# Graph layer kernel: keys, queries and prefix ahead of the compaction, sooner normalising, Z stores in quarters, dense comparisons

## The reference

```python
h = maximum(layernorm(x), 0)
semb, oemb = h[src] @ tokeys.T, h[src] @ toqueries.T
dots = sum(semb * relations[rel] * oemb, axis=1) / 128
values = exp(dots)
fr = src + n * rel
values = values / segment_sum(values, fr)[fr]
output = segment_sum(values[:, None] * h[dst], fr).reshape(16, n, 128)
weights = einsum('rb,bij->rij', comps, bases_w)
out = x + relu(einsum('rij,rnj->ni', weights, output))
```

## Time and profile before

| what | value |
|---|---|
| median of 3 runs | 2487.49 us (2487.05 to 2491.51) |
| profiled execution, its time | 2487.54 us |
| its span in the trace | 2485.8 us |
| PE busy over the span | 1327.6 us (53%) |
| DVE busy | 1336.7 us (54%) |
| ACT busy | 454.1 us (18%) |
| POOL busy | 1613.0 us (65%) |

### The profile page before, as it was taken

The page is one execution under the profiler, slowest core; times in us unless marked ns, Lnnn a source line. Parts: engine busy times, 40 slices in busy tenths (PEclk is TensorE's granted clock), DMA queues, the critical chain, the costliest instruction groups (busy, mean ns, idle before and its releaser), DMA issues.

```text
span 2485.8 us, 30053 instructions
## 1 busy us (share of the span) xinstructions
PE 1327.6 (53%) x9063; PEld 1000.5 (40%) x9113; DVE 1336.7 (54%) x2311; ACT 454.1 (18%) x868; POOL 1613.0 (65%) x1828
## 2 busy tenths in 40 slices
PE   2888988345453535454454545463545454454443
PEld 2665666234242424334342434342434344343433
DVE  7888888474545454454545454545454444545450
ACT  3555555210101011111101010101011111111010
POOL 3122222377777777777777777777777777777775
PEclk8999999666666767676666666666767676666666
DMA  4333333122222222222222222222222222222222
GB/s 124 139 139 127 134 139 137 53 54 56 54 56 54 55 54 56 54 55 54 56 55 54 56 54 56 54 56 54 56 54 56 54 56 54 55 54 56 55 54 41
DMA packets 77959, 170.30 MB, mean 69 GB/s; under 512 B 29796, under 2 KB 45148, under 8 KB 71511
## 3 DMA queue, kind: packets, MB, share of 16 engines
q0 software_dynamic: 52576, 106.12, 17.1%
q1 hardware_dynamic: 25010, 63.79, 7.0%
q10 hardware_dynamic: 352, 0.14, 0.0%
HBM read 112.99 MB, written 57.82 MB: 69 GB/s over the span
## 4 chain that ended last, share of the span: by engine, by line
POOL 59%; issue 21%; PE 15%; DMA 2%; DVE 1%; POOLq 1%; ACT 1%; SPq 0%; ACTq 0%; DVEq 0%
POOL arena L456 59%; PE bank L1112 7%; PE bank L1097 3%; PE bank L1065 1%; ACT H L907 1%; POOLq L448 1%; DMA bucket_streams<-REC,IDXW 1%; PE bank L1087 1%; PE bank L1104 1%; PE bank L1078 0%; DMA stage<-in_edge_type 0%; PE bank L1105 0%; PE bank L1225 0%; DVE stats L555 0%; PE bank L1123 0%
## 5 line engine op out<-in xcount | busy, mean ns | idle before, releaser
L456 POOL DMA_INDIRECT arena<-Z_messages,IDX x1593 | 1504.0, 944 | 495.3 <-issue 485.1
L1225 PE MATMUL bank<-arena 128*128 128x128 f32 x3528 | 514.7, 320 | 747.0 <-DMA arena<-Z_messages,IDX 747.0
L1225 PEld LDWEIGHTS bank<-arena 128*128 128x128 f32 x3528 | 506.8, 235 | 757.3 <-issue 757.3
L763 DVE SCALAR_TENSOR_TENSOR O<-bank,X 128x128 f32<-128x128 f32 x49 | 14.3, 292 | 725.4 <-PE bank L1225 725.4
L1015 ACT COPY pay_all<-bank 128x1024 bf16<-128x1024 bf16 x147 | 108.0, 807 | 1368.1 <-PE bank L1192 1359.5
L755 DVE TENSOR_TENSOR arena<-stage,bank 128x512 f32<-128x512 bf16 x441 | 267.7, 678 | 0.2 <-PE bank L1213 0.2
L419 POOL DMA_INDIRECT bucket_streams<-REC,IDXW x50 | 52.1, 1042 | 310.8 <-ACT REC L950 296.9
L698 DVE TENSOR_TENSOR stage<-bank,NLF 128x4608 bf16<-128x4608 f32 x49 | 242.4, 4947 | 0.0
L1182 PE MATMUL bank<-stage,OHR 128*128 128x512 bf16 (+1 forms) x392 | 181.4, 626 | 36.0 <-DVE arena L755 25.7
L1213 PE MATMUL bank<-pay_all 128*128 128x256 bf16 x882 | 136.5, 284 | 114.5 <-DVE arena L755 109.7
L1112 PE MATMUL bank<-WT,HT 128*128 128x512 f32 x392 | 186.9, 617 | 0.0
(11 more groups left out here) (177 smaller groups left out, 1465.2 us busy)
## 6 DMA issues: line engine op xcount, KB each, us to landing
Z_messages<-stage SPq DMA_DIRECT2D x48, 1024.0 KB, 3.9
arena<-Z_messages,IDX POOLq DMA_INDIRECT x1593
X<-in_x SPq DMA_DIRECT2D x4, 768.0 KB, 13.0
out<-O SPq DMA_DIRECT2D x48, 64.0 KB
arena<-in_L_gnn_bases_w SPq DMA_DIRECT2D x1, 1024.0 KB, 15.3
bucket_streams<-arena SPq DMA_DIRECT2D x1, 882.0 KB
bucket_streams<-bucket_streams SPq DMA_DIRECT2D x49, 18.0 KB
RL<-bucket_streams SPq DMA_DIRECT2D x49, 18.0 KB
```

Source lines behind the costliest of these rows:

```text
L456: g.indirect_dma_start(Gbuf[par][:, k, :], None, Z, bass.IndirectOffsetOnAxis(IDX[par][:, k:k + 1], 0))\
L1225: mm = t_.matmul(bank[2][:, 0:EMB], OW[:, k, :], Gbuf[par][:, k, :], start=(k == 0), stop=(k == G - 1))
```

## The change

1. On PE, `compact` of a step stands behind `keys_queries` and `prefix`.
2. On ACT, `copy_so` and `copy_prefix` stand ahead of `copy_d`, and `normalise(i + 1)` stands between the second and the third message copy.
3. `store_z` issues four DMAs of 512 columns, each as soon as its piece is copied; the semaphores of the stores count 64 for a block instead of 16.
4. ACT writes an unpaired copy q1 of the bucket numbers. The comparisons and additions for LOC run over single values, half as many elements; the reader of LOC broadcasts it to pairs.
5. Behind the loop, PE's matmul for the ends stands ahead of the last `records`, ROWI is made in bank 7 in place of bank 3, and two waits (`rec_sb`, `v`) stand behind it.

```diff
-        LOC2 = sb("LOC2", [EP, NCOL, 2], F16)
+        LOC = sb("LOC", [EP, NCOL], F16)
+        q1 = sb("q1", [EP, NCOL], F16)
...
             def store_z(i, par, skip, n=P):
-                sp.wait_ge(s["z_sb"], i * 4 + 4)
                 zr = Z[bass.ds(i * (P * R) + skip * R, n * R), :].rearrange("(p r) i -> p (r i)", r=R)
-                sp.dma_start(zr, ZS[par][0:n, :]).then_inc(zst[par], 16)
+                for k in range(4):
+                    sp.wait_ge(s["z_sb"], i * 4 + k + 1)
+                    sp.dma_start(zr[:, k * 512:(k + 1) * 512], ZS[par][0:n, k * 512:(k + 1) * 512]).then_inc(zst[par], 16)
...
-            by_group = lambda ap: ap.rearrange("p (g j) two -> p g j two", j=GW)
-            q_group, local = by_group(q2[:]), by_group(LOC2[:])
+            by_group = lambda ap: ap.rearrange("p (g j) -> p g j", j=GW)
+            q_group, local = by_group(q1[:]), by_group(LOC[:])
+            dve.wait_ge(s["dense"], 1)
...
-                    v.tensor_tensor(equal_at(d), q_group[:, :, d:GW, :], q_group[:, :, 0:GW - d, :], ALU.is_equal)\
+                    v.tensor_tensor(equal_at(d), q_group[:, :, d:GW], q_group[:, :, 0:GW - d], ALU.is_equal)\
                         .then_inc(s["loc"], 1)
                 if d > 2:
                     dve.wait_ge(s["loc"], 2 * d - 3)
-                    v.tensor_tensor(local[:, :, d - 1:GW, :], local[:, :, d - 1:GW, :], equal_at(d - 1), ALU.add)\
+                    v.tensor_tensor(local[:, :, d - 1:GW], local[:, :, d - 1:GW], equal_at(d - 1), ALU.add)\
...
+                if k == 0:
+                    a.activation(q1[:], whole, ACT.Copy).then_inc(s["dense"], 1)
...
-                if dyn(i) or 1 <= i <= NCH:
-                    copy_d(i - 1, 1 - par)
-                if ahead:
-                    copy_prefix(i + 1, 1 - par)
                 if dyn(i) or i < NB:
                     copy_so(i)
-                    copy_z(i, par)
+                if ahead:
+                    copy_prefix(i + 1, 1 - par)
+                if dyn(i) or 1 <= i <= NCH:
+                    copy_d(i - 1, 1 - par)
+                if dyn(i) or i < NB:
+                    copy_z(i, par, 0, 2)
                 if dyn(i) or i + 1 < NB:
                     normalise(i + 1)
+                if dyn(i) or i < NB:
+                    copy_z(i, par, 2, 4)
...
-                if dyn(i) or 1 <= i <= NCH:
-                    compact(i - 1, 1 - par)
                 if dyn(i) or i < NB:
                     keys_queries(i, par)
                 if ahead:
                     prefix(i + 1)
+                if dyn(i) or 1 <= i <= NCH:
+                    compact(i - 1, 1 - par)
...
-            run_steps(pe, step, NCH + 1)
+            run_steps(pe, step, NCH)
             pe.wait_ge(s["s8_sb"], NCH)
             pe.wait_ge(s["ends"], 2)
             t_.matmul(bank[0][0:NB, 0:2], both[:], ENDS[:], start=True, stop=True).then_inc(s["ends_mm"], 1)
-            pe.wait_ge(s["rec_sb"], NCH)
-            pe.wait_ge(s["v"], NCH)
+            step(NCH + 1, (NCH + 1) % 2)
+            pe.wait_ge(s["ncount"], NCH)
```

More of the change, by code:

```diff
@@ L144, in program @@
         own8 = late[:, G // 2 * P + 2 * P:G // 2 * P + 2 * P + 16 * P].bitcast(F32).rearrange("p (t n) -> p t n", t=8)
-        same = [pay_all[0:EP, p, 0:2 * NCOL // GW * (GW - 1)] for p in range(2)]
+        same = [pay_all[0:EP, p, 0:NCOL // GW * (GW - 1)] for p in range(2)]
         DS = [sb(f"DS{p}", [WIN, 2 * NS], F16) for p in range(2)]
@@ L206, in program @@
         names = """const x_in0 x_in1 x_in2 x_in3 x_in4 w_in bases_in edges_in kq_t kq_sb wt_mm wt_sb comps_d edge edges_done
-            dup loc stat varr stdd ln ohb s8 s8_sb bt bt_sb ncount own fold half m_sum rk ohs idxw mx pos pay d_mm d_sb rec_mm rec_sb scat
+            dup dense loc stat varr stdd ln ohb s8 s8_sb bt bt_sb ncount own fold half m_sum rk ohs idxw mx pos pay d_mm d_sb rec_mm rec_sb scat
             h th ht so_mm so_sb prod z_mm z_sb zst0 zst1 zrow v ends ends_mm nt nt_mm nt_row join sp_go marks_sb marks_st
@@ L438, in _ @@
             run_steps(pool, step, NCH + 1)
[L440 to L441 removed]
+            pool.wait_ge(zst[0], 64 * ((NB + 1) // 2))
+            pool.wait_ge(zst[1], 64 * (NB // 2))
             pool.wait_ge(s["zrow"], 16)
@@ L608, in ranks @@
                     dve.wait_ge(s["ohs"], i)
-                v.tensor_tensor(RK2[:], RK16[:].unsqueeze(2).broadcast_to([EP, TC, 2]), LOC2[:, bass.ds(i * TC, TC), :],
+                v.tensor_tensor(RK2[:], RK16[:].unsqueeze(2).broadcast_to([EP, TC, 2]), LOC[:, bass.ds(i * TC, TC)].unsqueeze(2).broadcast_to([EP, TC, 2]),
                                 ALU.add).then_inc(s["rk"], 1)
@@ L660, in _ @@
             dve.wait_ge(s["nt_mm"], 1)
-            v.tensor_copy(ROWI[:], bank[3][0:1, 0:4 * NB + 1]).then_inc(s["nt_row"], 1)
+            v.tensor_copy(ROWI[:], bank[7][0:1, 0:4 * NB + 1]).then_inc(s["nt_row"], 1)
             dve.wait_ge(s["nt_row"], 1)
@@ L955, in copy_rec, with copy_z @@
                     a.copy(stats[0:1, 0, 0:1], stats[0:1, 0, 1:2]).then_inc(s["v"], 1)
-            def copy_z(i, par):
-                for k in range(4):
+            def copy_z(i, par, lo, hi):
+                for k in range(lo, hi):
                     act.wait_ge(s["z_mm"], i * 4 + k + 1)
@@ L990, in _ @@
             for i in range(4):
-                step(i, i % 2, (i // 2) * 16)
+                step(i, i % 2, (i // 2) * 64)
             with act.Fori(2, (NB - 1) // 2) as j:
-                step(j * 2, 0, j * 16)
-                step(j * 2 + 1, 1, j * 16)
+                step(j * 2, 0, j * 64)
+                step(j * 2 + 1, 1, j * 64)
             for i in range(NB - 1, NCH + 2):
-                step(i, i % 2, (i // 2) * 16)
+                step(i, i % 2, (i // 2) * 64)
             act.wait_ge(s["nt_row"], 1)
@@ L1150, in _ @@
             t_.matmul(bank[0][0:NB, 0:2], both[:], ENDS[:], start=True, stop=True).then_inc(s["ends_mm"], 1)
+            step(NCH + 1, (NCH + 1) % 2)
+            pe.wait_ge(s["ncount"], NCH)
+            pe.wait_ge(s["nt"], 10)
+            t_.transpose(bank[7][0:1, 3 * NB + 1:4 * NB + 1], POS[0:NB, NCH:NCH + 1], identf[0:NB, 0:NB])
+            t_.matmul(bank[7][0:1, 0:NB], NT[:, 1:2], identf[0:NB, 0:NB], start=True, stop=True)
+            for p in range(2):
+                t_.matmul(bank[7][0:1, (1 + p) * NB:(2 + p) * NB], NT[:, 2 + p:3 + p], upto16[:], start=True, stop=True)
+            t_.matmul(bank[7][0:1, 3 * NB:3 * NB + 1], NT[:, 4:5], upto16[:, NB - 1:NB], start=True, stop=True)\
+                .then_inc(s["nt_mm"], 1)
+            pe.wait_ge(s["nt_row"], 1)
             pe.wait_ge(s["rec_sb"], NCH)
             pe.wait_ge(s["v"], NCH)
-            pe.wait_ge(s["nt"], 10)
-            t_.transpose(bank[3][0:1, 3 * NB + 1:4 * NB + 1], POS[0:NB, NCH:NCH + 1], identf[0:NB, 0:NB])
-            t_.matmul(bank[3][0:1, 0:NB], NT[:, 1:2], identf[0:NB, 0:NB], start=True, stop=True)
-            for p in range(2):
-                t_.matmul(bank[3][0:1, (1 + p) * NB:(2 + p) * NB], NT[:, 2 + p:3 + p], upto16[:], start=True, stop=True)
-            t_.matmul(bank[3][0:1, 3 * NB:3 * NB + 1], NT[:, 4:5], upto16[:, NB - 1:NB], start=True, stop=True)\
-                .then_inc(s["nt_mm"], 1)
-            pe.wait_ge(s["nt_row"], 1)
             bad = pe.value_load(ROWI[0:1, 3 * NB:3 * NB + 1], min_val=0, max_val=16 * NB)
```

14 lines of the change are left out of this document (7 added, 7 removed).

## The result

The changed kernel takes 2463.34 us (median of 4 runs, 2462.47 to 2463.82); the kernel before, run beside it, takes 2487.27 us (4 runs, 2486.23 to 2491.51). The ratio is 0.990, with a 95% interval of 0.9883 to 0.9917, a small gain but clear of the noise. The gain is 24 us, where 49 were forecast, and the time is 1.3 us above the upper end of the range. The profiled execution takes 2462.47 us, its span 2460.8 us, 25.0 us less than before.

A forecast was written before the change was run, and what follows sets the result against it. POOL's gathers stay as they are, so only the time before the first gather counts, mostly the loop's ring. 2487.5 - 40 (loop) - 4.9 (set-up) - 4.4 (behind the loop) = 2438.2 us; range 2428 to 2462.

The forecast's parts named there:

- What bounds the kernel: Whole kernel: POOL's gathers, some 2000 us from 478.76 on, stay unchanged; only the time before the first gather counts.
- The ring: Loop: PE's work, a message copy, a normalise, then PE again, every 8.035 us; without the wait for H, 7.2.
- lower bound of 7.06: Loop: the shortest step the forecast allowed, set by PE's own list, worth 46 us gained.
- The hidden wait of ACT: Loop, on ACT: SO waits for POOL's product until T + 3.1, hidden with 0.3 us to spare before the message copy.
- POOL paces the loop: Rival, loop: the product comes 0.7 us later than counted, 47 steps give back 19 us, 2457 us; chance 0.12.
- PE's new order: Loop, on PE: keys and queries asked for sooner wait for HT, costing up to 0.1 us a step.
- The set-up: Before the loop, on DVE: half the elements for LOC's comparisons and additions save 4.9 us.
- bound of no gain: Set-up: at one element a cycle LOC takes 10.2 us, what it is now, so nothing is saved.
- slow comparisons: Rival, set-up: the dense comparisons run at one element a cycle, 2443 us in all; chance 0.15.
- The stores: Loop, on SP: four DMAs take under 2 us of a 7.2 us step; cost nothing, gain nothing.
- Behind the loop: After the loop: rows of 2 KB leave a quarter of the store's delay, 3.4 us a scatter; 4.4 us gained.
- first interval: First to second transpose: the transpose idles 1.07 us there; 1 us gained, counted within the loop's 40.

The follow-up runs named there:

- e2: The kernel before with only the normalise moved between the second and third message copy: 2435.77 us, ratio 0.9792, step 6.968 us.
- e1: The changed kernel with a second SO buffer, so ACT's copy waits for the product of two blocks ago: 2446.25 us, ratio 0.9833.
- e3: The changed kernel with DVE's reduction (offsets) moved ahead of the second payload: 2446.88 us, ratio 0.9836.
- e5: The changed kernel with PE's compaction back ahead of keys, queries and prefix: step 7.599 us, 3112.89 us on a slower chip, ratio 0.9803.
- e10: e1 with ACT's copies of REC and V moved behind the relu that makes HT: 2438.98 us, ratio 0.9805, step 7.095 us.
- e6: The changed kernel with ACT's old order of DS, prefix and SO: step 7.250 us, 3102.22 us on a slower chip, ratio 0.9769.
- e4: The changed kernel with one store for a block instead of four: 2464.03 us, ratio 0.9907, step 7.605 us.
- e8: e2 with the last store of 106 rows cut into 96 and 10: 3110.0 us on a slower chip, ratio 0.9779.
- e7: The changed kernel with LOC shifted by one 16-bit element in its tile: 3127.26 us, one run on a slower chip.
- e11: The same kernel as e8, run again beside a kernel before of 2487.27 us: 2428.38 us, ratio 0.9765.

## Why the prediction was wrong

**What bounds the kernel: right.** The gathers didn't change (1504.2 and 495.4 us), and the time moved by what the first gather moved, 25.5 us.

**The ring and the early normalise: right.** The idle time for H is gone, and with nothing else changed (e2) the step is 6.968 us, 0.09 below the lower bound of 7.06.

**The hidden wait of ACT: the step that failed.** The forecast put SO's wait at T + 3.1, messages at T + 4.37, "with 0.3 us to spare". In the step above T, the start of the transpose, is 255.28, and the product ends at 259.36, T + 4.1. It is late by 1.0 us. REC came where it was forecast (T + 0.44 against 0.43), the scatter's start as well; the rest is 0.49 us on the scatter and 0.44 us on the product. Both lengths had been carried over from the earlier trace rows, although the forecast moved them to another time against DVE's list, beside the second payload and the next one-hots. The first message copy then starts at 260.20, T + 4.92, 0.55 us behind the T + 4.37 at which it was to be wanted, and the step is 7.61 us in place of 7.2; e1 puts POOL's part of that at 0.36. e1 (the wait taken out, 7.25) and e3 (the stretch moved elsewhere, 7.28) show the cause from both sides. This is the rival "POOL paces the loop" in its place and its price: it said 0.4 us a step given back and 2457; the rest of the 2463 comes from the set-up and the scatters, below. It had a chance of 0.12 for too narrow a reason, that REC moves back; the scatter and the product were never asked what runs beside them.

**PE's new order: cost low.** "Up to 0.1 us a step" was said of the wait for HT. Behind POOL's ring it can't be seen (e5), but in e1, where the step is 7.25, the wait is 0.26 us a step and the new order costs 0.28 against e2 (e10 gets 0.155 of it back). The forecast of 7.2 us agrees with the 7.25 of e1 and e6, the loop that POOL doesn't hold, but in part by luck: PE's list alone takes 6.97 us and not 7.06 or more, and the wait is longer than was said.

**The set-up: mis-sized.** 4.9 us were forecast and 2.6 measured. The comparisons run at the rate that was taken or, over odd rows, up to 0.12 us above it. The additions with odd rows don't come near it: 1.06, 1.04 and 1.06 us for rows of 5, 3 and 1 elements, and 1.27 for L539 with rows of 7. At two elements a cycle and 0.15 us fixed, as forecast, they would be 0.67, 0.46, 0.25 and 0.88, together 2.2 us less, nearly all of the missing 2.3. The bound of no gain was right to keep; the chance of 0.15 for slow comparisons was put on the wrong operand.

**The stores: right in the loop** (e4), and SP had room for four.

**Behind the loop: mis-sized.** The store on few engines was read rightly and e8 confirms it, but "a quarter" of the delay for a quarter of the row wasn't. The first two scatters took 6.53 and 6.00 us in place of 3.4, the last two 2.23 and 2.31. The gain is 0.8 us in place of 4.4. The delay follows the length of the rows only weakly. By the Trainium skill, DMA: Bandwidth & Descriptors, Queues, rings and completion order, as the forecast read it, it should have; e4 against the change doesn't bear that out.

**The sum.** The differences to the forecast are 39.2 - 20.1 in the loop, 4.9 - 2.6 in the set-up, 4.4 - 0.8 behind the loop, 1 - 2.1 in the first interval and 0.5 in the last part: 24.4 us, against 24.3 between 2438.2 and the profiled execution's 2462.47.

**What stays open.** What in the store of 106 rows sets a delay of 3.7 to 5.2 us that a shorter row leaves nearly as it is; why rows of LOC with an odd start or length cost a flat time; and why the first interval gained 2.1 us in place of 1, which no run looked at.

## What to carry to other kernels

When an edit moves work in time, look at what it will now run beside, not only at what it waits for: durations read in the old place hold only there, and here GpSimd's grew by 0.4 to 0.8 us beside a VectorE operation with two inputs (scatter, product and POS). Make each reordering alone: here the one that released a wait was worth 52 us, and the two made with it gave more than half of that back: 0.36 us a step because on ACT a copy that waits for another engine was put ahead of copies that don't, and 0.28 because on PE work was moved to where its input isn't ready yet. And count the rows of a store: as 106 rows in one DMA the last store cost 7 us behind the loop that it didn't cost as 96 + 10.

## What the runs showed of the hardware

- A GpSimd scatter or product that starts while VectorE runs an operation with two inputs is held: the scatter ends 0.9 us behind the end of that operation (1.53 us in place of 1.04), the product 0.3 us behind it (0.90 in place of 0.46). Beside a reduction the scatter takes 1.04 us (e3). It is held though it is only the issue of a DMA.
- VectorE's 16-bit operations on an array of short rows (200 rows at a pitch of 8) take a flat 1.04 to 1.09 us for 1 to 6 elements a row when a row begins at an odd element or has an odd length, and 0.51 to 0.78 us when neither is so (e7). With a dense output, an odd start of an input and an odd row cost no more than the next even row does (0.78 us for 5 as for 6, 0.58 us for 3 as for 4).
- While a store of 106 rows ran, DMA moved 54 GB/s for 18 us, and the scatters issued meanwhile took 6.0 to 7.5 us; as 96 + 10 rows it was over within 7 us (221 GB/s in the first 3), one scatter took 4.2 us and the ones behind it 2.3 (e11). The size of the row, 2 or 8 KB, changed the delay by under a microsecond (e4).
- Four stores of a quarter block against one showed no difference in a step of 7.6 us (7.608 and 7.605).
